# Two edits to a six-layer decoder kernel: another order of work in the autocorrelation layer, and context products of cross attention in pieces of 32 columns

## The reference, cut to what matters

```python
x = ln(x + L0_attn(x))            # causal self attention, 32 heads of 16
x = ln(x + autocorrelation(x, ctx, ctx))   # the first stage of this change
x = ln(x + L0_moe_lora(x))
x = ln(x + L1_attn(x))            # ALiBi, normed q and k
x = ln(x + L1_xattn(x, ctx))      # the second stage: 16 heads of 96, 4 key/value groups, 256 keys
x = ln(x + L1_ffn(x))

def autocorrelation(Q, K, V):     # per head and channel, over the 128 positions
    corr = ifft(fft(Q) * conj(fft(K))).real
    w, idx = top_k(corr, 9);  w = softmax(w)
    out[t] = sum_i w[i] * V[min(idx[i] + t, L - 1)]
```

## Time and profile before

| | |
|---|---|
| runs | 933.66 us median (936.04, 933.66, 931.77) |
| profiled execution | 930.5 us, its span 928.7 us, mean TensorE clock 0.981 of full |
| PE busy | 861.7 us (93%), 8680 matmul records |
| PEld (weight loads) | 689.7 us (74%) |
| DVE, ACT, POOL busy | 589.4, 418.4, 269.6 us |
| L1131 (context products) | 1024 records, 52.3 us |
| L1002, L989 (shifted sums, lag spectra) | 64 and 32 records |

### The profile page before, as it was taken

One profiled execution on the slowest core, in us unless ns is written; L12 is line 12 of the kernel. 1 busy time (PEld: TensorE's weight loads), 2 busy tenths in 40 slices (PEclk: granted clock), 3 DMA queues, 4 the chain that ended last, 5 costly groups with the idle time before them and its releaser, 6 DMA issues.

```text
span 928.7 us, 21428 instructions
## 1 busy us (share of the span) xinstructions
PE 861.7 (93%) x8680; PEld 689.7 (74%) x8680; DVE 589.4 (63%) x1526; ACT 418.4 (45%) x1076; POOL 269.6 (29%) x316
## 2 busy tenths in 40 slices
PE   7999998996898989899999798899999999999995
PEld 5677776673444767677777587888989898889983
DVE  3555665466776666557776533997376747665775
ACT  4254434343565324345555343633545264436532
POOL 1122222277887541111223246760000100010001
PEclk9999999898999999899999999999999999999998
DMA  6400000132331010000000011230000010000001
GB/s 224 154 22 14 21 16 23 58 93 65 93 101 46 23 52 1 8 21 26 17 16 18 25 37 60 87 123 1 24 1 1 2 46 1 1 2 23 2 2 45
DMA packets 21233, 37.05 MB, mean 40 GB/s; under 512 B 3264, under 2 KB 7488, under 8 KB 20880
## 3 DMA queue, kind: packets, MB, share of 16 engines
q1 hardware_dynamic: 21088, 35.62, 12.4%
q10 hardware_dynamic: 48, 0.07, 0.0%
HBM read 29.16 MB, written 2.10 MB: 34 GB/s over the span
## 4 chain that ended last, share of the span: by engine, by line
PE 76%; DVE 13%; POOL 4%; issue 3%; ACT 2%; DMA 1%; SPq 1%; POOLq 0%; DVEq 0%; ACTq 0%
PE bank L746 17%; PE bank L747 15%; PE bank L748 15%; PE bank L867 6%; PE bank L1131 5%; PE bank L888 3%; DVE tank L2313 2%; PE bank L841 2%; DVE tank L2323 2%; PE bank L872 2%; PE bank L1002 1%; DVE tank L2099 1%; PE bank L826 1%; PE bank L765 1%; PE bank L1151 1%
## 5 line engine op out<-in xcount | busy, mean ns | idle before, releaser
L746 PE MATMUL bank<-wr,hTl 128*128 128x512 f32 (+3 forms) x472 | 190.4, 403 | 4.2 <-DVE wr L2028 2.1
L747 PE MATMUL bank<-wr,hTh 128*128 128x512 f32 (+3 forms) x472 | 181.2, 384 | 0.0
L748 PE MATMUL bank<-wr,hTh 128*128 128x512 f32 (+3 forms) x472 | 181.2, 384 | 0.0
L2099 DVE TENSOR_REDUCE tank<-bank 128x4 f32<-128x512 f32 x128 | 82.4, 686 | 58.0 <-PE bank L841 58.0
L746 PEld LDWEIGHTS bank<-wr,hTl 128*128 128x128 f32 (+1 forms) x472 | 89.9, 191 | 28.8 <-issue 8.6
L1389 ACT ACTIVATE pT<-bank 128x512 f32<-128x512 f32 x128 | 70.1, 605 | 87.8 <-PE bank L841 87.7
L748 PEld LDWEIGHTS bank<-wr,hTh 128*128 128x128 f32 (+1 forms) x472 | 90.0, 191 | 17.4
L747 PEld LDWEIGHTS bank<-wr,hTh 128*128 128x128 f32 (+1 forms) x472 | 90.3, 191 | 15.3 <-issue 1.2
L867 PE MATMUL bank<-qk 32*128 32x128 f32 x1024 | 76.8, 289 | 19.0 <-DVE tank L2099 8.7
L867 PEld LDWEIGHTS bank<-qk 32*128 32x128 f32 x1024 | 64.5, 191 | 35.6 <-issue 24.7
L872 PE MATMUL bank<-qk 32*128 32x128 f32 x1024 | 76.0, 287 | 0.3 <-DMA qk<-tank 0.3
(11 more groups left out here) (235 smaller groups left out, 1845.3 us busy)
## 6 DMA issues: line engine op xcount, KB each, us to landing
raw<-w_qkv_dram SPq DMA_DIRECT2D x12, 256.0 KB, 3.0
raw<-w_xq_dram SPq DMA_DIRECT2D x16, 192.0 KB, 2.4
raw<-w_xo_dram SPq DMA_DIRECT2D x12, 256.0 KB, 2.7
x_all<-x_dram SPq DMA_DIRECT2D x8, 256.0 KB, 6.8
cin<-ctx_dram SPq DMA_DIRECT2D x8, 256.0 KB, 3.4
cin<-ctxT_dram SPq DMA_DIRECT2D x8, 256.0 KB, 2.8
out_dram<-x_all SPq DMA_DIRECT2D x8, 256.0 KB, 2.0
qk<-extra_dram SPq DMA_DIRECT2D x124, 16.0 KB
```

The source lines that it names most:

```text
L746: mm(dst, lhs[1], rhs[0], start=start, stop=False)
L747: mm(dst, lhs[0], rhs[1], start=False, stop=False)
L748: return mm(dst, lhs[0], rhs[0], start=False, stop=stop)
L2099: v.tensor_reduce(nm[b % 2][:, at:at + KT], s_bank[n][:, :].rearrange("p (m t) -> p m t", m=KT), AX, ALU.max, negate=True).then_inc(max_re ...
```

## The change

In the autocorrelation stage the orders of five engines change; the last two norms of the self attention go from POOL to ACT (POOL keeps the one-column power and the shift); the pieces 3 to 10 are made two turns later and pieces 9 and 10 after the last turn; in cross attention every head's 96 columns become three pieces of 32, so 24 products in place of 16 for each slot and group. The diff (unchanged lines left out):

```diff
 SyncE
-                fetch(pieces, 0, 0, PIECES_A0, slice(b + 2, b + 3))
-            fetch(pieces, 0, 0, PIECES_A0, slice(B + 2, B + 4))
+                if b < 3:
+                    fetch(pieces, 0, 0, PIECES_A0, slice(b + 2, b + 3))
+                elif b >= 5:
+                    fetch(pieces, 0, 0, PIECES_A0, slice(b, b + 1))
+            fetch(pieces, 0, 0, PIECES_A0, slice(B, B + 4))
 PE, mixture_period(k)
-                if k > 0:
-                    lag_weights_to_lags(k - 1)
-                    lag_spectrum(k - 1)
+                lag_weights_to_lags(k - 1)
+                if k + 2 < B:
+                    x_spectrum(k + 2)
+                elif k == B - 2:
+                    pe.wait_ge(ctxf_ready, 2 * B)
+                    x_to_features(0, 0, MOE, 2)
+                lag_spectrum(k - 1)
+                if k + 2 < B:
+                    even_spectrum(k + 2)
                 if k + 1 < B:
                     correlation(k + 1)
                 if k + 2 < B:
-                    x_spectrum(k + 2)
-                    even_spectrum(k + 2)
                     odd_spectrum(k + 2)
                 if k == B - 1:
-                    pe.wait_ge(ctxf_ready, 2 * B)
                     pe.wait_ge(lagf_ready, 2 * (B - 1))
-                    each(x_to_features, 0, MOE, 2)
+                    x_to_features(0, 1, MOE, 2)
 PE, cross attention
+            def quarters(tile):
+                return [(row + part, j, first + part) for at, row, j, first, n in places if at == tile for part in range(0, n, NARROW)]
-                        for _, row, j, first, n in [at for at in places if at[0] == tile]:
-                            ins = mm(bank[s][0][row:row + n, tile * P:(tile + 1) * P],
-                                     xv[s][:, t * NKV + g * XD + first:t * NKV + g * XD + first + n],
+                        for row, j, first in quarters(tile):
+                            at = t * NKV + g * XD + first
+                            ins = mm(bank[s][0][row:row + NARROW, tile * P:(tile + 1) * P], xv[s][:, at:at + NARROW],
                                      xpT[s][:, (2 * j + t) * P:(2 * j + t + 1) * P], start=t == 0, stop=t == 1)
 PE, before and after the turns
             correlation(2)
+            even_spectrum(3)
             x_spectrum(3)
-            even_spectrum(3)
             odd_spectrum(3)
 ...
-            each(base, 0)
+            base(0, 0)
             lag_weights_to_lags(B - 1)
+            base(0, 1)
             lag_spectrum(B - 1)
 ACT
+            def last_rows(b):
+                s = b % 2
+                act.wait_ge(ln_rstd[s], 2)
+                av(x_all[:, b, :], x_all[:, b, :], ACT.Identity, bias=st[s][:, SHIFT], scale=st[s][:, RSTD]).then_inc(x_ready[s], 1)
             def mixture_period(k):
-                lag_weights(k - 1)
+                if k > 2:
+                    lag_weights(k - 1)
 ...
+                if k == 2:
+                    last_rows(B - 2)
+                    last_rows(B - 1)
+                else:
+                    piece_hi(k + 1)
                 if k >= 4:
                     norm_mixture(k - 4)
-                piece_hi(k + 3)
 ...
             lag_weights(0)
+            x_spectrum(2)
             o_split(0, B - 1)
             lag_weightsT(0)
-            x_spectrum(2)
 ...
             lag_spectrum(0)
+            lag_weights(1)
+            context_spectrum(3, 0)
             x_spectrum(3)
-            for i in range(2):
-                context_spectrum(3, i)
-            piece_hi(4)
+            context_spectrum(3, 1)
             for k in range(2, B):
                 mixture_period(k)
+            piece_hi(B + 1)
 ...
             each(gate_exp, 0)
+            piece_hi(B + 2)
 POOL
-                    pool.wait_ge(x_ready[1], seq(TRIPS - 1, A0))
+                    pool.wait_ge(branch_added, batch(0, B - 1))
+            def last_rstd(b):
+                s = b % 2
+                pool.wait_ge(ln_var[s], seq(b // 2, A0))
+                nc.gpsimd.tensor_tensor(st[s][:, RSTD], st[s][:, MV][:, 1:2], half[:, 0:1], ALU.pow).then_inc(ln_rstd[s], 1)
+                pool.wait_ge(ln_rstd[s], 1)
+                hold()
+                nc.gpsimd.tensor_scalar(st[s][:, SHIFT], st[s][:, MV][:, 0:1], st[s][:, RSTD], -1.0, ALU.mult, ALU.mult
+                                        ).then_inc(ln_rstd[s], 1)
             def mixture_period(k):
 ...
+                if k == 2:
+                    last_rstd(B - 2)
+                    last_rstd(B - 1)
                 shift_products(k - 1)
-                piece(k + 3)
+                piece(k + 1)
 ...
-            norm_rows(A0, B - 2)
             cross_products(2)
-            piece(3)
             shift_products(0)
-            norm_rows(A0, B - 1)
             rows_without_partner(3)
-            piece(4)
             for k in range(2, B):
                 mixture_period(k)
+            piece(B + 1)
             rstd_mixture(B - 4)
             rstd_mixture(B - 3)
             shift_products(B - 1)
             rstd_mixture(B - 2)
+            piece(B + 2)
             piece(B + 3)
```

More of the change, by code:

```diff
@@ L462, in normed @@
             per_trip = {MOE: 2, XA: 1}[y]
-            return nth(trip, per_trip, j, {MOE: 0, XA: 2}[y] * TRIPS)
+            return nth(trip, per_trip, j, {MOE: 0, XA: 2}[y] * TRIPS + 2)
         def one_of(trip):
```

## The result

The changed kernel takes 920.03 us (median of 4 runs, 918.27 to 921.42), against 934.85 us for the kernel before on the same chip (4 runs, 931.77 to 937.38). The ratio is 0.9862, with a 95% interval of 0.9828 to 0.9895. Two later comparisons gave 0.9866 [0.9823, 0.9909] and 0.9864 [0.9834, 0.9893]. So the change is worth some 12.9 us (9.8 to 16.1 by the first interval); the two medians themselves are 14.8 us apart, inside that interval. The forecast was 12.2 us, 921.5 us by the median, in a range of 915 to 928.

The account below looks back on a forecast made before the run. PE's own work was taken as the bound (76% of the wait chain), other engines mattering where PE idles. Context products 5.2 plus autocorrelation 7.0 gave 12.2 us: 918.3 from the profiled 930.5, 921.5 from the 933.66 median; range 915 to 928.

Parts of the forecast that it names:

- Context products: Cross attention: 32-column pieces leave one width change per pair of trains instead of four; 5.2 us saved, bounds 0 to 7.5.
- rival D: Context products: neighbouring groups sharing a moving operand don't stream abreast; +2.1 us a pair, 956 us in all; chance 0.05.
- weaker form: Context products: about 60 cycles per matmul added to streaming for the new records; 0.8 us a pair, sum near 928.
- Autocorrelation: Autocorrelation stage: reordered engines fill waits in the ring of five; 7.0 us saved, bounds 2.5 to 11.7.
- The walk: Autocorrelation stage: the profile's clock followed with old durations in the new order, from correlation(2) through the turns and behind.
- The clock stays at 1.00 near 220: At correlation(2): with about 2.4 us idle PE's granted clock should stay at 1.00, where it had been 0.50.
- in place 4.03 us after SyncE's issue: Ahead of correlation(2): the DMA swap takes 4.03 us from issue, ending at 215.0, so PE starts at 217.6, 3.5 us sooner.
- Turn 4 begins 8.6 us sooner: Autocorrelation turns 2 and 3: x_spectrum fills PE's wait, 10.1 us a turn; turn 4 begins at 246.0 instead of 254.60.
- Turn 6 and behind it: Autocorrelation's end: context_spectrum(7) waits for shift_products(4), cutting the gain to 6.8 us; base(0, 1) filling a gap makes it 7.6.
- rival A: Autocorrelation: the engine ring binds harder, DVE's sums always stopping behind denser POOL; this part gives 2.5, 926.0 us; chance 0.18.
- The 0.28 us row: Autocorrelation: profile row taken to show one DVE sum without POOL at work, against 1.35 us with POOL at work.
- Rival C: Only one part works: clock falls again near 216 to 226, 3 us a time, or DVE takes part 1; 929.7 us; chance 0.09.

Follow-up runs that it names:

- third profile of the changed kernel: The changed kernel rerun unaltered beside the kernels with added edits: 921.0 us, ratio 0.9864 against the kernel before.
- profile without half clock: Changed kernel with the context-product edit undone, so only the autocorrelation changes against the kernel before: 926.08 us, ratio 0.9927.
- second profile of the changed kernel: The changed kernel rerun with no edit, on the same chip as the kernel before: 919.13 us, ratio 0.9866.
- TensorE's old order: Changed kernel with TensorE's orders inside the turns and at the stage's end put back to those of the kernel before: 922.06 us, ratio 0.9869.

## Why the prediction was right, and where its steps were not

**Context products, 5.2 us forecast, 4.6 to 4.8 measured.** Group by group the first profile came as worked out: nothing in group 0 of trips 1 to 3; 0.40 to 0.46 us in the pairs of groups 1 and 2 (0.41 forecast); 0.42 to 0.48 in group 3 (0.47 forecast). What is missing in it is one pair, trip 0's group 1: ahead of the next one PE waited 0.91 us for VectorE's copies instead of 0.43. In the third profile of the changed kernel that wait is 0.34 and the pair wins 0.45, so this is a matter of the execution. The width change as a cost of its own, 0.16 us, and the streaming of narrow groups side by side both hold. The 2.83 us pair excludes rival D. It excludes as well the reading in which the 60 cycles of the Trainium skill's TensorEngine Tiling (Array Packing), section Instruction Overhead, come on top of the streaming; by the page itself a product of one column takes as long as one of 60, and these have 128. (The 956 of rival D and the 928 of its weaker form are counted from the profiled execution, the other rivals' times from the median, which is 3.2 us more.) That VectorE holds group 0, which I only read off the order of its rows, was tried by moving its copies and is shown.

**Autocorrelation, 7.0 forecast, 6.8 measured** (4.3 to 8.1 in single profiles). The walk is right as far as the swap takes what it was taken to take: in the profile without half clock, put on the clock of the kernel before (1.80 us later), correlation(2) starts at 217.54 (217.6 forecast), correlation(3) at 228.95 (228.8) and layer 4 at 323.67 (324.5). The 1.00 us wait for POOL ahead of correlation(4) was forecast too. Three steps are not right.

- *The clock stays at 1.00 near 220.* It did in three of the five profiles of this code, behind 2.25 to 2.44 us of idle time (2.4 was forecast), and fell in two, behind 3.38 and 3.77. The step that failed there is the swap "in place 4.03 us after SyncE's issue": it took 4.00 to 4.17 in the first three, 5.02 and 5.49 in the others. One row of before was not enough to give it a range.
- *Turn 4 begins 8.6 us sooner.* By the profile without half clock it began 8.12 us sooner net, by the first one 6.05. Turn 4 itself is 10.0 us, as forecast (10.1), turn 3 with POOL's wait 11.35, and no idle time is left before the lag spectrum in turns 2 to 5.
- *Turn 6 and behind it: 6.8, then 7.6 with the gap at the base.* Turn 6 began 7.6 to 9.7 us sooner: turns 4 and 5 won 1.6 us together, where about 0 was forecast, and ScalarE's wait for the shift products bound less than I thought (1.14 us). What bound instead isn't in my walk: `lag_sums(6)` beside POOL's shift products, and mixture 3's sum behind it. Of 4.3 us lost inside turn 6 in the first profile, 2.3 are that wait and 1.8 the half clock behind it; in the profile without half clock 2.6 us were lost. The gap at the base gave 0.9 to 1.0 us in these two (0.8 forecast). The argument against rival A, that the later turns' sums meet only POOL's short operations, was wrong: VectorE's L2263 takes 19.7 us in this stage in the first profile, where it took 14.0 before (28 operations each, mean 757 and 551 ns). The 0.28 us row wasn't taken with POOL idle either: POOL had an operation of one column under way, from 280.08 to 280.69 us.

So rival A's mechanism was real and cost 2.3 us of TensorE's time, less than the 4.5 that it was priced at. Rival C's falling clock was real as well and takes 1.8 us a time, not 3, in some executions. That 7.0 came within 0.2 us of the measured 6.8 is in part luck: the gain of turns 4 and 5 was put too low, VectorE's wait and the falls of the clock were left out, and over several executions these cancel. The later weight pieces were hidden, as forecast: layer 4's first row waits 0.29 us, for ScalarE.

Left open in part: why the swap takes 4.0 us in some executions and 5.5 in others. In the two profiles with the long swap the DMA engines were 0.83 and 0.79 busy from 213 to 215 us, and in the one with the shortest 0.80, so their load doesn't tell them apart. The third of SyncE's four issues does in most cases, here in the changed kernel's first profile and in that of the autocorrelation part alone:

```profile
210.47 1.79 SPq L710 DMA_DIRECT2D spec<-spec  x1
```
```profile
210.79 0.52 SPq L710 DMA_DIRECT2D spec<-spec  x1
```

It took 1.71 to 1.90 us in three of the four profiles with a swap over 5 us, and held the fourth issue, L711, back to 3.39 to 3.58 us behind the first, where it otherwise starts 2.21 behind it. A 16 KB packet of the instruction queue, q8, falls into this stretch in every profile, and in all eleven with the new order of ScalarE and POOL the third or fourth issue ends 0.37 to 0.40 us behind the end of it. That SyncE waits there for its own instructions is likely by these times, not shown; the fourth long swap, 5.02 us in the second profile of the changed kernel, had a third issue of 0.52 us and stays unexplained.

## What to carry to other kernels

When the waits of a ring of engines are filled one after another, look for the small operation that frees a buffer and stands last in its engine's order: 0.7 us of VectorE's work behind 5 us of stalled work held TensorE. Move it ahead in every turn where the buffer is reused, since moved in one turn alone the wait appears in the next. Before an idle time of TensorE is filled, follow what comes behind: here the idle time moved to the next operand and the clock fell there instead. And a single profile of such a stage may show half the gain or all of it: here by how long one swap by DMA took and where the clock fell. Before a kernel is called undisturbed, read the granted clock of the whole stage, not only where it fell the last time.

## What the runs showed of the hardware

- Thirty-two-column weights in four groups stream at 26.7 ns a record (96 in 2.56 us) when neighbouring groups share their moving operand, as when they don't (32 in 0.85 us).
- In this stage an idle time of TensorE of 2.25 to 2.44 us left the granted clock at 1.00 and one of 3.38 to 3.83 us was followed by 0.50; but 2.31 us ahead of `shifted_sum(5)` was followed by 0.50 in two profiles and by 1.00 in three. Ahead of `shifted_sum(6)` 1.22 us was followed by 0.50 in two profiles (from 291 and 287 us) and by 1.00 in the other three of that code; and with TensorE's old order 1.93 us ahead of correlation(3) was followed by 0.50. The idle time alone doesn't settle it.
- Small VectorE operations can pay most for POOL's work. One of 128x4 elements, 0.17 us beside an operation of one column on POOL, took 2.15 in turn 6, up to the end of POOL's second product (269.74). Not all pay: the four MAX8 just ahead of it (266.68 to 267.57) took 0.89 us beside POOL's products, their length in every turn. VectorE's and POOL's rows of the changed kernel:

```profile
267.61 2.15 DVE L2244 TENSOR_SCALAR stats<-stats 128x4 f32<-128x4 f32 x1
...
280.57 0.17 DVE L2244 TENSOR_SCALAR stats<-stats 128x4 f32<-128x4 f32 x1
...
267.24 1.27 POOL L1916 TENSOR_TENSOR tank<-xf,tank 128x512 f32<-128x512 f32 x1
268.47 1.27 POOL L1917 TENSOR_TENSOR tank<-xf,tank 128x512 f32<-128x512 f32 x1
```
